# Deformable convolution network: image stored by column modulo four, offsets loaded per chunk

## The reference

```
for each of 4 blocks:
    h      = relu(3x3 convolution of the block's input, 32 -> 32 channels)
    offset = 3x3 convolution of h, 32 -> 18 channels      (y and x for each of 9 taps)
    x      = relu(deform_conv(h, offset, w, b))
    from the second block on, the block's input is x + the input of the block before
final: offset from concat(x, normalised input), 64 channels;  out = deform_conv(concat, offset, w, b)
result = input + out

deform_conv: for each output pixel and each of 9 taps k, the image is read bilinearly at
    (row + ky + offset_y, column + kx + offset_x), zero outside; then a 288 -> 32 product
```

## Time and profile before

| | |
|---|---|
| median of 3 runs | 6885.23 us (6860.79 to 6908.06) |
| the profiled execution, its own time | 6814.77 us |
| its span from the first to the last instruction | 6813.0 us |
| mean granted clock of TensorE in it | 0.796 of full speed |
| busy: TensorE, VectorE, ScalarE, GpSimd | 77%, 44%, 41%, 17% |
| DMA packets' time, as a share of 16 engines' span | 53.3% on SP's queue |

### The profile page before, as it was taken

One profiled execution on the slowest core, in us unless ns is written; L12 is line 12 of the kernel. 1 busy time (PEld: TensorE's weight loads), 2 busy tenths in 40 slices (PEclk: granted clock), 3 DMA queues, 4 the chain that ended last, 5 costly groups with the idle time before them and its releaser, 6 DMA issues.

```text
span 6813.0 us, 210332 instructions
## 1 busy us (share of the span) xinstructions
PE 5270.7 (77%) x73160; PEld 3746.3 (55%) x73160; DVE 2989.2 (44%) x5831; ACT 2803.4 (41%) x7035; POOL 1134.7 (17%) x655
## 2 busy tenths in 40 slices
PE   3888688688688768868858868876777777678887
PEld 2555455355455545545535545554656566566776
DVE  3444454355355345445535534533334342344444
ACT  1554354255355345435525525542323232233333
POOL 0221222122022122112202202211101010111110
PEclk8778787688788878878868877887788788788888
DMA  5553553355255255345435525547666665778875
GB/s 152 75 75 56 79 80 60 70 80 81 56 77 79 57 79 78 55 81 81 71 65 78 78 56 77 77 91 106 78 77 84 79 80 83 116 91 96 96 90 77
DMA packets 615113, 544.03 MB, mean 80 GB/s; under 512 B 90160, under 2 KB 570160, under 8 KB 613040
## 3 DMA queue, kind: packets, MB, share of 16 engines
q1 hardware_dynamic: 614576, 536.57, 53.3%
HBM read 468.16 MB, written 68.12 MB: 79 GB/s over the span
## 4 chain that ended last, share of the span: by engine, by line
PE 51%; issue 21%; DMA 12%; ACT 6%; SPq 4%; DVE 3%; ACTq 1%; POOL 1%; POOLq 0%; PEldq 0%; PEld 0%; DVEq 0%
PE P L502 20%; PE PS L516 17%; PE PS L528 13%; DMA HB<-off_store 11%; SPq L355 4%; ACT SMP L676 2%; DVE A L828 2%; ACT XC L707 2%; ACT DIST L693 2%; PE P L474 1%; ACTq L704 0%; DMA H<-gn_store 0%; DMA gn_store<-X 0%; POOL HL L1000 0%; DMA X<-x_dram 0%
## 5 line engine op out<-in xcount | busy, mean ns | idle before, releaser
L828 DVE TENSOR_TENSOR A<-P,XC 121x384 f32<-121x384 f32 (+1 forms) x4608 | 2412.5, 555 | 3006.6 <-ACT XC L707 1595.6
L707 ACT ACTIVATE XC<-P 121x384 f32<-121x384 f32 (+1 forms) x4608 | 1961.1, 443 | 2903.3 <-PE P L502 2876.1
L502 PE MATMUL P<-HL,SEL 32*121 32x384 f16 (+1 forms) x21504 | 2355.4, 345 | 835.7 <-POOL HL L1000 393.6
L502 PEld LDWEIGHTS P<-HL,SEL 32*121 32x121 f16 (+1 forms) x21504 | 1341.2, 132 | 1632.7 <-issue 879.8
L516 PE MATMUL PS<-A,VT 121*32 121x144 f32 (+1 forms) x32768 | 1467.0, 335 | 124.1 <-issue 95.1
L516 PEld LDWEIGHTS PS<-A,VT 121*32 121x32 f32 (+1 forms) x32768 | 1098.5, 127 | 468.4 <-issue 238.0
L528 PE MATMUL PS<-SMP,CW 128*128 128x128 f32 x6912 | 1100.3, 316 | 301.7 <-ACT SMP L676 300.9
L528 PEld LDWEIGHTS PS<-SMP,CW 128*128 128x128 f32 x6912 | 963.6, 219 | 529.5 <-ACT SMP L676 428.2
L998 POOL CAST HL<-DIST 128x1152 f16<-128x1152 f32 x320 | 366.2, 1144 | 4394.1 <-DVE DIST L844 4110.0
L1000 POOL TENSOR_TENSOR HL<-DIST,HL 128x1152 f16<-128x1152 f32 x320 | 760.0, 2375 | 129.7 <-issue 73.9
L676 ACT ACTIVATE SMP<-PS 128x288 f32<-128x288 f32 x1536 | 639.2, 416 | 24.0 <-PE PS L516 22.7
(11 more groups left out here) (55 smaller groups left out, 826.4 us busy)
## 6 DMA issues: line engine op xcount, KB each, us to landing
HB<-off_store SPq DMA_DIRECT2D x1280, 144.0 KB, 5.7
VT<-ht_store SPq DMA_DIRECT2D x1024, 128.0 KB
VT<-ht_store SPq DMA_DIRECT2D x2816, 44.0 KB
ht_store<-A SPq DMA_DIRECT2D x80, 256.0 KB, 3.6
off_store<-FOFF SPq DMA_DIRECT2D x160, 128.0 KB, 2.5
ht_store<-H SPq DMA_DIRECT2D x6, 1444.0 KB, 19.4
A<-x_dram SPq DMA_DIRECT2D x2, 2048.0 KB, 10.9
gn_store<-X SPq DMA_DIRECT2D x2, 2048.0 KB, 26.3
```

Source lines behind the costliest of these rows:

```text
L502: mm = nc.tensor.matmul(dst, SEL[q, table, 0:sh.npos], hats, start=part == 0, stop=part == 1)
L707: nc.scalar.activation(XC[0:sh.npos, slot, 0:sh.size], P[0:sh.npos, 2 * slot, 0:sh.size], ACT.Copy).then_inc(x_ready, 1)
L828: return nc.vector.tensor_tensor(dst, y, x, ALU.mult)
```

## The change

The transposed image is kept in DRAM in four **lanes**: pixels whose column is j modulo 4 stand together, lane after lane. The eight blocks of a chunk are 4 columns apart, so one window position's eight pixels are contiguous: 4 KB in kind 0 and 8 KB in kind 1. A chunk's windows come in four DMAs, one per lane, of 33, 33, 33 and 22 partitions in kind 0 and 64 each in kind 1. `transposes` takes every fourth column; the selection tables follow the new order of positions.

Offsets are stored with the x rows at row 16, and loaded for one half at a time: four DMAs of 32 partitions, each half with a semaphore of its own. The source's outermost dimension is now the two axes, then 16 repeats. SP issues a chunk's offsets two chunks ahead. Those of chunks 0 and 1 are loaded in the first part of the step, after unit 0's stores have landed and ahead of unit 1's stores; `distance`, `clamp` and the hats of chunk 0 move there too, each on its engine ahead of what followed there.

In the loop of groups y comes first and is copied by ScalarE (`YC`); y has three banks, x four. `PS` is one bank for samples and sums; a chunk's (in kind 1 a batch's) eight units are sampled in three parts (3, 3 and 2) after g = 2, 5 and 8, and `deform` runs whole after g = 10. The choice of the kind is nested, and one barrier per step is gone. The renames and the fallback's edits are left out of the diff.

```diff
@@ names and sizes
+LANES = 4
+LANE_COLS = HP // LANES
+LANE = HP * LANE_COLS
-SHEETS = UNIT_ROWS * HP // 128
-BANKFULS = (SHEETS + 3) // 4
+SHEETS = UNIT_ROWS * LANE_COLS
+BANKFULS = (SHEETS + 127) // 128
+AXIS = 16
@@ class Shape
+        if kind == 0:
+            self.lanes = [(0, 33 * j, 3 if j < 3 else 2) for j in range(LANES)]
+        else:
+            self.lanes = [(j // 2, 64 * (j % 2), 4) for j in range(LANES)]
-        self.parts = [(w, s) for w in range(0, self.blocks, 2) for s in range(sources)]
-        self.sum_spots = [8, 10] if len(self.parts) < 8 else [9, 10]
+        units = [(w, s) for w in range(self.blocks) for s in range(sources)]
+        count = {4: 2, 8: 3, 16: 6}[len(units)]
+        edges = [(len(units) * n + count - 1) // count for n in range(count + 1)]
+        self.parts = [units[a:b] for a, b in zip(edges, edges[1:])]
+        self.after = {2: [3, 7], 3: [2, 5, 8], 6: [0, 2, 4, 5, 7, 8]}[count]
+        self.sum_after = 10
@@ tensors and credits
-        ht_store = [nc.dram_tensor(f"ht_store{n}", (HP, HP, n, 128), F32) for n in (1, 2)]
-        SLOTS = 3
+        ht_store = [nc.dram_tensor(f"ht_store{n}", (LANES, HP, LANE_COLS, n, 128), F32) for n in (1, 2)]
+        Y_SLOTS, X_SLOTS = 3, 4
-        P = ctx.enter_context(nc.psum_tensor("P", [128, 6, 512], F32))
-        PS = ctx.enter_context(nc.psum_tensor("PS", [128, 2, 512], F32))
+        P = ctx.enter_context(nc.psum_tensor("P", [128, Y_SLOTS + X_SLOTS, 512], F32))
+        PS = ctx.enter_context(nc.psum_tensor("PS", [128, 512], F32))
-        credit = [(x_ready, SLOTS), (product_done, SLOTS), (y_full, 1), (ps_full, 2), (ps_free, 2), (res_done, 2), (turn, 1)]
+        credit = [(y_ready, Y_SLOTS), (product_done, X_SLOTS), (x_full, 1), (ps_full, 2), (ps_free, 1), (res_done, 2), (turn, 1)]
@@ sampling(): the three kinds
-            with eng.If(kind == 1):
-                body(Shape(1, sources))
-            with eng.If(kind > 1):
-                fallback(Shape(2, sources))
-            barrier(eng, bar_count + 1)
-            clear_step(eng, bar_count + 2, clears)
+            with eng.Else():
+                with eng.If(kind == 1):
+                    body(Shape(1, sources))
+                with eng.Else():
+                    fallback(Shape(2, sources))
+            clear_step(eng, bar_count + 1, clears)
@@ SP: loads
-            def load_offsets(band):
+            def load_offsets(band, half):
                 for i in range(IMG):
-                    for axis in range(2):
-                        at = band * BAND_SIZE + (i * 2 * CH + axis * TAPS) * CPX
-                        src = bass.AP(off_store.ap().tensor, at, [[0, ROWS], [CH * CPX, 2], [1, TAPS * CPX]])
-                        q = CH * i + ROWS * axis
-                        sp.dma_start(HB[q:q + ROWS, :, :], src).then_inc(hb_full, 16)
+                    at = band * BAND_SIZE + (2 * i + half) * CH * CPX
+                    src = bass.AP(off_store.ap().tensor, at, [[AXIS * CPX, 2], [0, AXIS], [1, TAPS * CPX]])
+                    sp.dma_start(HB[CH * i:CH * (i + 1), half, :], src).then_inc(hb_full[half], 16)
-            def load_windows(sh, buf, corner):
-                for r in range(sh.win):
-                    tile, first = divmod(r, sh.win // sh.tiles)
-                    src = bass.AP(ht_store[sh.sources - 1].ap().tensor, corner + r * (HP * sh.sources * 128),
-                                  [[sh.sources * 128, sh.win], [BLK * sh.sources * 128, BLOCKS], [1, sh.sources * 128]])
+            def load_windows(sh, buf, corners):
+                width = sh.sources * 128
+                size = BLOCKS * width
+                for corner, (tile, first, columns) in zip(corners, sh.lanes):
+                    src = bass.AP(ht_store[sh.sources - 1].ap().tensor, corner, [[LANE_COLS * width, sh.win], [width, columns], [1, size]])
+                    sp.dma_start(VT[first:first + sh.win * columns, buf, tile * size:(tile + 1) * size], src).then_inc(vt_full[buf], 16)
-                load_offsets(0)
-                load_windows(sh, 0, corner(0, 0))
-                with sp.Fori(0, BANDS - 1) as band:
-                    sp.wait_ge(abs_done, 2 * band + 2)
-                    load_offsets(band + 1)
-                    free_windows(2 * band + 1)
-                    load_windows(sh, 1, corner(band, 1))
-                    free_windows(2 * band + 2)
-                    load_windows(sh, 0, corner(band + 1, 0))
+                def next_offsets(c, band, half):
+                    sp.wait_ge(abs_done, c - 1)
+                    load_offsets(band, half)
+                def next_windows(c, band, half):
+                    sp.wait_ge(ps_full, (c - 1) * sh.ps_uses + 1)
+                    load_windows(sh, half, corners(band, half))
+                load_windows(sh, 0, corners(0, 0))
+                load_windows(sh, 1, corners(0, 1))
+                next_offsets(2, 1, 0)
+                next_offsets(3, 1, 1)
+                with sp.Fori(0, BANDS - 2) as pair:
+                    next_offsets(2 * pair + 4, pair + 2, 0)
+                    next_windows(2 * pair + 2, pair + 1, 0)
+                    next_offsets(2 * pair + 5, pair + 2, 1)
+                    next_windows(2 * pair + 3, pair + 1, 1)
@@ SP: step(), after the stores of unit 0's offsets
+                    if unit == 0:
+                        for slot in range(OFF_SLOTS):
+                            sp.wait_ge(off_stored[slot], 32)
+                        load_offsets(0, 0)
+                        load_offsets(0, 1)
@@ TensorE: transposes(), batch()
-                    for r in range(count):
-                        at = HP + 128 * (first + r)
+                    at = HP + LANES * first
+                    for lane in range(LANES):
+                        columns = source[:, at:at + LANES * count].rearrange("p (q r) -> p r q", r=LANES)[:, lane, :]
-                        pe.wait_ge(x_ready, n + 1)
-                        spread(sh, g, b, half, x_table, 2 * slot).then_inc(x_full, 1)
+                        pe.wait_ge(y_ready, n + 1)
+                        spread(sh, g, b, half, y_table, g % Y_SLOTS).then_inc(y_full, 1)
                         pe.wait_ge(product_done, n + 1)
-                        for tile in range(sh.tiles):
-                            mm = spread(sh, g, b, half, y_table + tile, 2 * slot + 1, sh.size * tile)
-                        mm.then_inc(y_full, 1)
+                        for tile, table in enumerate(x_tables):
+                            mm = spread(sh, g, b, half, table, Y_SLOTS + g % X_SLOTS, sh.size * tile)
+                        mm.then_inc(x_full, 1)
@@ ScalarE: step(), ahead of sampling()
+                distance(0, 0)
@@ VectorE: step(), in the loop over the eight offset items
+                    if n == IMG:
+                        clamp(0)
@@ GpSimd: step(), ahead of the reduction
+                hats(0, 0)
```

287 lines of the change are left out of this document (137 added, 150 removed).

## The result

The changed kernel takes 6249.79 us (median of 4 runs, 6222.56 to 6264.4), the kernel before took 6873.01 us beside it (4 runs, 6830.16 to 6908.06): ratio 0.9091, 95% interval 0.9028 to 0.9155. The forecast was 6735 with a range of 6480 to 7200, so the gain is more than four times the one forecast. The profiled execution has a span of 6240.0 us and a mean granted clock of 0.842 (0.796 before). Runs of one kernel differ by some 2% with the granted clock, ratios leave the slower ones out, and the one profile that is of a slower run is that of e17_parts_apart (6785.65 us, the longest of its four).

What follows compares the result with a forecast made beforehand. Two DMA engines carrying the offset rows were to become the bound at 14.3 us a chunk; +79 - 40 - 50 - 40 - 100 = -151 us on the profiled 6814.77 gave 6664, as a median 6735, range 6480 to 7200.

Steps and rivals of the forecast that it cites:

- What bounds the kernel now: Short steps: TensorE leads; each HB wait costs 1.7 us plus slow-clock chunks behind it, mean 13.98 us a chunk.
- rival 1: Offset load runs on all 16 engines, TensorE bounds at full clock, 11.3 us a chunk: median 5915; chance 14%.
- 14.3 us: Short steps: work per chunk of the two busiest DMA engines, 11.9 for offset rows plus 2.4 for windows.
- Engine count: New offset load, source outermost dimension 2, runs on two DMA engines; a DMA share of about 0.12 between window peaks.
- Kind-0 term, +79 us: Short steps' chunks: 14.3 against 13.98 us, +0.32 us x 31 chunks x 8 steps.
- The lower bound, 13.4: Short steps' chunk: least time, 13.1 us and a little for completions; upper bound 18.3.
- no longer matters: Short steps: the slow clock after a wait costs nothing, since a 17-us chunk lets the two engines catch up.
- Start, -40 and -50: Start of sampling: early offset loads save 5 us in each of eight steps and 25 in each final step.
- Ends, -40: Between steps: jumps over unused kinds and a barrier go, -4 us in each of ten steps.
- Final steps, -100: Final steps: larger window rows mean fewer instruction-fetch gaps, -50 us each; bounds 0 and -130, or +60 each.
- Rival 2: Two engines need more than 14.9 us per chunk, slower than before: 7155 at 16.0 us, 7735 at 18.3; chance 22%.
- Banks, parts, order: nothing below 14.3: TensorE's chunk from the new banks, parts and order stays at 10.8 to 11.8 us, costing nothing below 14.3.

Runs made afterwards that it cites:

- e17: e15 with the short steps' four parts after g = 2, 3, 5 and 6 instead of two after 2 and two after 5: 6734.93 us, ratio 0.983.
- e8: e5 with offsets loaded per chunk, two chunks ahead, as eight DMAs of sixteen rows: 5894.24 us, ratio 0.857.
- e1: Changed kernel with its per-chunk offset load as eight DMAs with outermost dimension sixteen instead of four with two: 5729.46 us, ratio 0.842.
- e9: Changed kernel with offsets of images 2 and 3 loaded with outermost dimension sixteen, those of images 0 and 1 still with two: 5775.19 us, ratio 0.841.
- e7: e1 without the early start (first offsets loaded and chunk 0's hats made after the barrier): 5827.49 us, ratio 0.848.
- e5: Kernel before with only the image's new layout in lanes and its four window DMAs a chunk: 6575.0 us, ratio 0.966.
- e3: Changed kernel without the early start (first offsets loaded and chunk 0's hats made after the barrier): 6315.65 us, ratio 0.927.
- e12: e8 with the changed kernel's early start, nested choice and one barrier less: 5682.12 us, ratio 0.829.
- e15: e1 with three x and two PS banks, two-unit parts in all steps (short: two after g = 2, two after 5), short steps' sum divided: 5575.68 us, 0.812.
- e16: e15 with the final steps' sum in two pieces after g = 9 and 10 instead of one after g = 10: 5581.42 us, ratio 0.822.

## Why the prediction was right or wrong

**What bounds the kernel now: right, and not followed.** It said that the wait for HB "costs its 1.7 us and then the slow chunks behind it". e8 takes the wait away, and the short steps lose 544 us. The sum used this only in rival 1 and, at 14.3 us, left it out of the forecast.

**Engine count: right.** Share 0.13 between peaks. e1 and e9 show that these two engines are the bound in the short steps, and that half of the load is free in the loop. The Trainium skill's "DMA: Bandwidth & Descriptors" ("Why a DMA increments its semaphore by 16 and not by 1") takes the engine count from the slowest dimension; here 2 gives a share of 0.13, and the trace agrees.

**Kind-0 term, +79 us: the first of the two steps that failed, and the larger, 263 us off.** The mechanism was right and its size wrong, so that the sign turned. 14.3 us was 11.9 + 2.4. Measured: 11.6 for the rows (25.5 GB/s for 24.8), and 13.2 for a chunk from chunk 2 to 31, which leaves 1.6 for the windows. Over 232 intervals 13.2 for 14.0 is -184 us. What failed is the choice of 2.4 us for the windows and the 0.3 us of rate, 1.1 us in all, on a term where a tenth of a microsecond is 23 us. The lower bound, 13.4, is a little above the measured 13.2; its 13.1 follows from no row, since the fastest rates of the earlier trace rows give 11.9 + 1.8 = 13.7. That the clock "no longer matters" was right: chunks from 11.1 to 18.1 us alternate in the changed kernel, and each step's mean lies between 13.2 and 13.3.

**Start, -40 and -50: the mechanism right, size -26 and -10.** Moved back by 39.5 us, the steps forecast were the load of half 0 landing at 657.5 (656.85), FOFF item 4 at 659.5 (658.81), chunk 2's read 5 us earlier (3.7: 49.4 us after the last convolution for 53.1) and GpSimd's gap of 7.55 us moving to chunk 1's hats (7.82). The final steps' -25 each was wrong: chunk 1 to 2 takes 28.6 us there for 19.3 in the first of them; that its windows of 2 MB queue behind the offsets is argued, not shown. With sixteen engines, where the forecast said -12, chunk 2's DIST comes 22 us earlier than in the kernel before (e1: 244 us for 422 in eight steps).

**Ends, -40:** -23 in the nine gaps between steps, 2.2 to 3.4 us in eight of them. The -4 was a little high.

**Final steps, -100: the other step that failed, 247 us off.** The mechanism is borne out as far as the lanes go (fewer and shorter gaps with larger packets), the size was -347. The bound "-130 (the half of all)" is about the half of the first step's gaps alone (238 us; the second has 111 more), and counted a gap as its own length. Three things were missed. Most of the gaps went, 238 us to 46 in the first step. With them went low clock, 396 us to 85 there, and 78 us of TensorE's busy time. And more than the windows counted: of the 397 us from the kernel before to e7, lanes bring 181 (e5), offsets by the chunk 87 (e8) and the rest 129; the two-engine load takes 40 to 60 of it back (e1 to the changed kernel 41, e7 to e3 59). What makes the 129 stays open: e12, with the nested choice, one barrier less and the early start, gains 50 on e8; e15 excludes the larger parts, e16 the place of the sum.

**Rival 1** (sixteen engines, 5915) is e1: 0.842 x 6885 = 5798. The price of that rival was good, and the rows had told it apart rightly. **Rival 2** needed over 14.9 us a chunk; 25.5 GB/s excludes it. **"Banks, parts, order: nothing below 14.3"** held as cover; uncovered they are worth 1.1% together, one barrier less included (e8 to e7), all of it in the final steps: the short ones get 74 us dearer. The places of the parts alone can cost 21% (e17).

## What to carry to other kernels

Where stretches of low clock begin behind a stall or a gap, price the busy time at the new clock too, and not only the stall. Keep the outermost dimension of every DMA's source at sixteen where the volume matters: here a two in its place cost 8% with two chunks of lead, and 33% without. And when moving TensorE's work closer together, look at the granted clock as well as at the waits: the same matmuls with two parts moved by one group ran at 0.60 to 0.73 in the loop instead of 0.97 to 0.99.

## What the runs showed of the hardware

- Two DMA engines alone, each writing rows of 4608 B, ran at 25.5 GB/s each, sixteen in a burst of the same rows at 8.1: two fifths of the total rate with an eighth of the engines. In e1, where sixteen engines carry a chunk's load among other transfers, a row took 0.27 us, 16.8 GB/s.
- TensorE's clock fell without any stall in front of it: in e17 it was busy 4.95 of 5 us at 1.00, and then stood at 0.50 for tens of microseconds. In the kernel before, the 78 low stretches of the short steps' loops begin 0.8 to 4.2 us behind a wait of ScalarE for HB. What decides it was not settled.
- The same loop ran at 11.6 us a chunk in some steps and at up to 12.1 in others, in e1 as in e7, by the share of chunks that hold a stretch of low clock (12.7 us for 11.1). What chooses between them is open.
- SP's issue of four offset loads took 3.7 to 8.5 us where they ran on two engines (800 to 900 us of the changed kernel), and eight took 3.9 us in e1: the slow issue was not the bound. That it is a sign of full DMA queues is argued.
